# Layer norm two batches ahead computed earlier in a batch, and the loops over batches of both layers written out

## The reference, cut to what matters

```python
x = L0_attn_x                                    # (16, 512, 128)
xn = _layernorm(x, axis=-1)
x = x + _L0_attn_ref(xn, ...) + _L0_ffn_ref(xn, router_w, w_fc, w_proj, shared_fc, shared_proj)
xn = _layernorm(x, axis=-1)
x = x + _L1_attn_ref(xn, ...) + _L1_ffn_ref(xn, W_r, W_k, W_v, mu_r, mu_k)

def _layernorm(x, axis=-1, eps=1e-05):
    m = jnp.mean(x, axis=axis, keepdims=True)
    v = jnp.var(x, axis=axis, keepdims=True)
    return (x - m) / jnp.sqrt(v + eps)
```

## Time and profile before

| | us |
|---|---|
| median of 3 runs (2136.6 to 2157.64) | 2152.94 |
| the profiled execution's own time | 2159.12 |
| its span in the profile | 2157.4 |
| first layer, from the first scores of body 0 to those of body 15 | 54.2 to 699.4 |
| second layer, from the first scores of body 16 to those of body 31 | 1132.7 to 2091.8 |
| mean granted TensorE clock | 0.836 |

### The profile page before, as it was taken

One profiled execution on the slowest core, in us unless ns is written; L12 is line 12 of the kernel. 1 busy time (PEld: TensorE's weight loads), 2 busy tenths in 40 slices (PEclk: granted clock), 3 DMA queues, 4 the chain that ended last, 5 costly groups with the idle time before them and its releaser, 6 DMA issues.

```text
span 2157.4 us, 41151 instructions
## 1 busy us (share of the span) xinstructions
PE 1757.5 (81%) x13440; PEld 1049.7 (49%) x13440; DVE 1312.3 (61%) x3161; ACT 848.8 (39%) x1597; POOL 603.2 (28%) x775
## 2 busy tenths in 40 slices
PE   2788888887888699999269878888787887888895
PEld 1465556555555489999123334333333433333432
DVE  2666665566566444444276767667676667767663
ACT  1333333333333133333115444444454544444553
POOL 1554454445543312121322222112222122221000
PEclk9899998999999889999656787787787787778776
DMA  3110011101110166666352323332223332233300
GB/s 81 30 42 26 26 34 33 34 26 35 30 38 21 49 199 210 213 209 212 77 98 56 70 51 72 72 78 57 63 49 78 71 77 50 64 58 65 65 7 10
DMA packets 118025, 152.92 MB, mean 71 GB/s; under 512 B 30004, under 2 KB 82356, under 8 KB 113204
## 3 DMA queue, kind: packets, MB, share of 16 engines
q1 hardware_dynamic: 102920, 119.73, 22.4%
q0 software_dynamic: 14976, 31.49, 5.0%
HBM read 109.53 MB, written 41.62 MB: 70 GB/s over the span
## 4 chain that ended last, share of the span: by engine, by line
PE 57%; DVE 21%; issue 8%; DMA 8%; ACT 3%; SPq 1%; POOL 1%; DVEq 0%; POOLq 0%; another core or an unknown queue 0%; ACTq 0%
DVE nmax L1140 7%; PE bank L1656 7%; PE bank L1485 6%; PE bank L1610 6%; PE bank L1601 6%; DMA out<-xr 5%; PE bank L1683 5%; PE bank L1470 3%; PE bank L1451 3%; PE bank L1467 3%; PE bank L1532 3%; DVE xn L836 2%; PE bank L1631 2%; PE bank L1391 2%; DVE rope L1125 2%
## 5 line engine op out<-in xcount | busy, mean ns | idle before, releaser
L1140 DVE TENSOR_REDUCE nmax<-bank 128x1 f32<-128x512 f32 (+3 forms) x704 | 431.9, 630 | 174.4 <-PE bank L1656 159.7
L759 ACT ACTIVATE P<-bank 128x512 f32<-128x512 f32 x640 | 365.0, 597 | 343.3 <-PE bank L1683 329.7
L1656 PE MATMUL bank<-KT,QT 76*128 76x512 bf16 (+3 forms) x1024 | 328.4, 382 | 176.0 <-DVE nmax L1140 149.3
L1683 PE MATMUL bank<-QT,KT 78*128 78x512 bf16 (+3 forms) x1024 | 307.0, 383 | 8.2 <-DMA QT<-shift_d 4.2
L1656 PEld LDWEIGHTS bank<-KT,QT 76*128 76x128 bf16 x1024 | 98.1, 113 | 400.7 <-DVE nmax L1140 323.8
L528 POOL TENSOR_TENSOR P<-P,tri 128x512 f32<-128x512 f32 x128 | 160.2, 1272 | 301.0 <-ACT P L671 300.8
L1485 PE MATMUL bank<-P,V 128*32 128x512 f32 (+3 forms) x2048 | 225.2, 523 | 0.0
L1089 DVE TENSOR_TENSOR hT<-hr 128x512 f32<-128x512 f32 x144 | 99.6, 692 | 109.7 <-ACT hr L728 109.7
L1683 PEld LDWEIGHTS bank<-QT,KT 78*128 78x128 bf16 x1024 | 115.8, 119 | 99.4 <-ACT P L759 34.0
L728 ACT ACTIVATE hr<-bank 128x512 f32<-128x512 f32 x144 | 86.0, 597 | 167.5 <-PE bank L1601 167.5
L571 POOL DMA_INDIRECT hT<-ys_d,idx x128 | 129.8, 1014 | 50.5 <-issue 45.9
(11 more groups left out here) (204 smaller groups left out, 2569.3 us busy)
## 6 DMA issues: line engine op xcount, KB each, us to landing
P<-in_fc SPq DMA_DIRECT2D x72, 256.0 KB, 2.6
P<-in_proj SPq DMA_DIRECT2D x72, 256.0 KB, 2.9
QT<-parts_d SPq DMA_DIRECT2D x96, 192.0 KB
parts_d<-parts SPq DMA_DIRECT2D x32, 384.0 KB, 2.8
P<-xs_d SPq DMA_DIRECT2D x72, 128.0 KB, 2.2
ys_d<-P POOLq DMA_DIRECT2D x72, 128.0 KB, 2.7
KT<-parts_d SPq DMA_DIRECT2D x64, 128.0 KB
KT<-parts_d SPq DMA_DIRECT2D x32, 192.0 KB
```

The source lines that it names most:

```text
L759: nc.scalar.activation(P[s % 2][:, u, :], bank[k % 2][:, :], ACT.Exp, scale=float(DH) ** -0.5).then_inc(s_sb, 1)
L1140: nc.vector.tensor_reduce(nmax[:, j, h:h + nh], bank[2 + k % 2][:, 0:nh * w].rearrange("p (h w) -> p h w", h=nh), AX.X, ALU.max, negate=Tr ...
L1656: ins = pe.matmul(bank[2 + k % 2][:, i * w:(i + 1) * w], QT[n.p][0:MROWS, h, j * 128:(j + 1) * 128], KT[n.p][0:MROWS, h, 0:w], start=True, ...
L1683: ins = pe.matmul(bank[k % 2][:, c:c + n], KT[b.p][0:SROWS, h, 128 * kb:128 * kb + 128], QT[b.p][0:SROWS, h, 128 * kb:T], start=True, stop ...
```

## The change

Two things are changed. The helpers `over_batches` and `over_layer2`, which every engine uses, now write out all bodies, with known batch numbers, in place of the loops; the loop over the experts' tiles stays. And in the first layer the layer norm of batch b+2 is placed earlier in body b: `ln_moments` on DVE after `cut(b, 1)`, `ln_root` on POOL after the scatter of sheet 1, and `ln` on DVE after `y_out(b, 0)`, in front of `rotate(b + 1, 1)`. The waits stay as they were. Lines behind the helpers move up by 10.

```diff
--- before.py
+++ after.py
@@ -282,13 +282,8 @@
 
         def over_batches(eng, body):
 
-            for p in range(2):
-                body(Turn(0, p), p == 0, False)
-            with eng.Fori(1, HALVES - 1) as i:
-                for p in range(2):
-                    body(Turn(i, p), False, False)
-            for p in range(2):
-                body(Turn(HALVES - 1, p), False, p == 1)
+            for n in range(B):
+                body(Turn(n // 2, n % 2), n == 0, n == B - 1)
 
         def value(eng, v):
 
@@ -304,13 +299,8 @@
 
         def over_layer2(eng, body):
 
-            for k in range(-2, 2):
-                body(Turn(HALVES, 0) + k)
-            with eng.Fori(HALVES + 1, 2 * HALVES - 2) as i:
-                for p in range(2):
-                    body(Turn(i, p))
-            for k in range(-4, 1):
-                body(Turn(2 * HALVES, 0) + k)
+            for n in range(L2 - 2, L2 + B + 1):
+                body(Turn(n // 2, n % 2))
 
         def over_tiles(eng, body):
 
@@ -543,8 +533,8 @@
                         mask(b, s, g)
                     if s < SHEETS - 1:
                         scatter(b, range(3 * s, min(3 * s + 3, 2 * J)))
-                if not (b.known() is not None and b.known() + 2 >= B):
-                    ln_root(b + 2)
+                    if s == 1 and not (b.known() is not None and b.known() + 2 >= B):
+                        ln_root(b + 2)
 
             ln_root(Turn(0, 0))
             ln_root(Turn(0, 1))
@@ -989,22 +979,24 @@
                     y_out(b + -1, 3)
                     normalise(b + -1)
                 cut(b, 1)
+                more = not (b.known() is not None and b.known() + 2 >= B)
+                if more:
+                    dve.wait_ge(x_loaded[b.p], (b + 2).own(16, 16))
+                    ln_moments(b + 2)
                 if not last:
                     rotate(b + 1, 0)
                 cut(b, 2)
                 if not first:
                     residual(b + -1)
                 y_out(b, 0)
+                if more:
+                    ln(b + 2)
                 if not last:
                     rotate(b + 1, 1)
                     feature(b + 1)
                 cut(b, 3)
                 if not last:
                     logits_out(b + 1)
-                more = not (b.known() is not None and b.known() + 2 >= B)
-                if more:
-                    dve.wait_ge(x_loaded[b.p], (b + 2).own(16, 16))
-                    ln_moments(b + 2)
                 y_out(b, 1)
                 if not last:
                     states(b + 1)
@@ -1014,8 +1006,6 @@
                     square_h(b, k)
                 if not last:
                     slots(b + 1)
-                if more:
-                    ln(b + 2)
 
             dve.wait_ge(ready_consts, 11)
             dve.wait_ge(x_loaded[0], 16)
```

## The result

The changed kernel takes 2175.46 us, the median of 4 runs (2170.64 to 2181.88), against 2145.0 for the kernel before (4 runs, 2136.6 to 2157.64): a ratio of 1.0146 with an interval of 1.0107 to 1.0185. It is slower by about 31 us. The profiled execution took 2181.88 against 2159.12, and the two spans differ by 22.8 us, 2180.2 against 2157.4.

A forecast was written before the change was run, and what follows sets the result against it. PE, busy 81% of the span, was taken as the bound. First layer +30.5 and second layer -28.5 gave +2.0 on the profiled 2159.12, so 2161; that execution being 6.2 above the median, 2155 us, range 2125 to 2188.

The forecast's parts named there:

- the two halves cancel: Whole kernel: first layer's +30.5 us and second layer's -28.5 nearly offset, giving 2155, own range 2133 to 2174; chance 0.50.
- rival 2: First layer: last scatters share DMA engines with whole-batch transfers, landing held back 2 us; +28 us, 2183; chance 0.23.
- rival 4: Both layers: writing out brings nothing, the trace's written-out bodies being quick for another reason; 2184, up to 2207; chance 0.07.
- The boundary: First layer, between bodies: with `ln` gone from a body's end, fourteen boundaries win 2.9 us each.
- The wait: First layer, mid-body: `ln` waits for POOL's last scatter; DVE 7.0 us late, PE idle 3.9 us before `project_v`.
- A full body at full clock: First layer: a body with the early `ln` takes 40.9 + 3.8 = 44.7 us.
- The clock term: First layer: PE's partly lower clock costs 0 to 0.8 us a body; 0.5 added, giving 45.2.
- The gain of writing out ... some 24 us: First layer: written-out bodies fall from 43.3 to about 41.3 us, already contained in the 40.9 used.
- The gap of 2.8 us at a jump: Loop jumps: PE idles 19.8 / 7 each; if only five jumps count, 14 us come back, forecast 2170.
- Body 0: First layer's first body: has the delay before `ln` but no gain at its start, +6.7 us.
- The second layer: Ten loop bodies, written out, take 62.7 us instead of 65.55: -28.5, bounds -22.5 and -38.5.
- Rival 3: First layer's bodies: 2 us of slack in the later half catches up the delay; 2119 to 2129; chance 0.20.

The follow-up runs named there:

- the third buffer: The changed kernel with three instead of two buffers for `xn` in the first layer, so `ln` overwrites rows sent a body earlier: 2104.49 us, ratio 0.9771 to the kernel before.

## Why the prediction was right, and where it was wrong

The forecast was 2155 with a range of 2125 to 2188; measured is 2175.46. The range holds it, but the heart of the forecast, that the two halves cancel (2133 to 2174), doesn't. The range was that wide for the sake of rivals 2 and 4, and neither came true as it was described, so that it holds is in part luck. Of the signs of being wrong that the prediction named, one came: seven of thirteen bodies lie over 47, and the bodies are not all alike.

- **The boundary.** Right. `turn_xn` waits for `xn` nowhere, and body 14, which has only this gain, takes 38.2 instead of 41.7. That is 3.5 and not 2.9; its clock went from 0.96 to 1.00 as well.
- **The wait.** Right in place and size. `ln` started 23.7 us after the body's first scores (132.59 - 108.9); the forecast had 24.0. Its last scatter was issued 21.3 us after them (130.22), and forecast at 21.3 (118.1 - 96.8). `ln` cost 1.12, forecast 1.11. PE waited 3.1 before `project_v`, forecast 3.9. The end of phi came 28.6 after the first scores (136.85 + 0.69 - 108.9), forecast 29.3 (126.1 - 96.8).
- **A full body at full clock**, 44.7: close, but not confirmed by the six bodies of 44.7 to 44.9, which ran at 0.92 and already hold some loss by the clock. With the pause partly filled a body of this order takes 44.0 at 1.00, so the forecast was some 0.7 too high, and that the shorter bodies hit it to 0.2 is luck.
- **The clock term.** This is the step that failed: "So the clock costs between 0 and 0.8 a body; I add 0.5: 45.2." Measured is a mean of 46.3 (601.3 / 13), that is 1.6 above 44.7, outside the bounds. Against the 44.0 of a body at full clock, the six shorter ones lose 0.8 and the seven longer ones 3.5, in the mean 2.3 where 0.5 was added. The bounds came from a comparison of the loop's bodies with body 1, less the jump gaps. They took the gaps as pure loss, and body 1's clock of 1.00 as what a written-out body has. The runs with the first layer written out show that neither holds: without the gaps every body has the pause for `xn`, where in the loop 8 of 12 had it, and more time at the lower level. With PE kept at work in that pause the old order's body falls from 44.0 to 41.3, so the pause and the clock behind it cost 2.7 us there, not 0.8; its bodies at a clock of 1.00 (40.7) are 3.7 shorter than body 8 at 0.88 (44.4). In thirteen bodies the forecast is 13.7 us short (601.3 - 587.6), of the 20.8 by which it missed the difference of the spans (22.8 - 2.0).
- **"The gain of writing out ... some 24 us"** in the first layer: it is not there in the old order, where the first layer loses 10.6. The sum didn't use this number, but the 40.9 of body 1 stands behind both: its clock of 1.00 is one that the old order, written out, doesn't keep: body 1 itself has 0.89 there, and body 8 has 0.88.
- **The gap of 2.8 us at a jump** (19.8 / 7) is a misreading: three of the seven waits are 0.6 us or less, and the four long gaps have a mean of 4.7. With that mean the prediction's five jumps give back 24 us instead of 14, and its other forecast, by jumps alone, would have been 2160 instead of 2170. The sum itself didn't use it.
- **Body 0**: +10.4 instead of +6.7. With the third buffer it takes 49.0 instead of 53.0, with `ln` behind the logits 44.7, against 42.6 before. So some 4 us are the wait; the rest goes with a lower clock (0.66, 0.71 and 0.77 against 0.78), and no run took it apart.
- **The second layer**: -24.6 in all instead of -28.5, inside its bounds. The ten bodies gave 18.7, 63.7 each and not 62.7; the edges 5.9, which weren't counted.
- **The rivals.** The forecast was +2.0 us between the profiled executions, and +22.8 came. The time came out on the side of rival 2, slower by 1.5%, but not by its mechanism: `ln` began 2.4 us after the issue of the last scatter (130.22 to 132.59), where that rival needed 4.1 or more. Rival 3 is refuted by the 44.8. Rival 4 is refuted for the second layer, by the run with that layer alone written out, 0.9924. For the first layer its claim came true in the old order: writing out brought nothing, and body 1 was quick in the trace for another reason, its clock.

As the Trainium skill has it ("Runtime: NRT & Kernel Launch", section "Instruction fetch mechanics"), a taken branch to code outside the window that is held stops execution until it is fetched, one reason why kernels prefer to be written out. The first half fits this case: the four gaps of 3.7 to 5.4 us at jumps are gone with the loops, though the traces don't show that a fetch fills them. The second doesn't hold for every loop: the first layer written out alone is slower by 0.9%.

The Trainium skill's lock of the port pair ("SBUF — State Buffer", section "Who interferes with whom") fits this case in five places: the four operations of `ln` take 3.03, 2.61 and 2.06 us beside a mask of POOL, 1.11 and 1.12 without one. The traces show that `ln` is slower beside a mask, not what holds it.

## What to carry to other kernels

Before a step is moved forward, list every wait it carries and ask of each when it is met at the new place; a wait on a buffer's last reader that never cost anything can become the longest of the body. Then move it to where the last of them is met and the engine is idle anyway: behind `logits_out` instead of in front of `rotate`, with its root one sheet later, the same layer norm made the kernel 3.7% faster together with the written-out loops, instead of 1.5% slower; with the loops kept it was 1.1% faster instead of 3.0% slower. And price a pause of PE by what follows it too: body lengths that come in two sorts with two clocks point to it, and repeating harmless matmuls in the pause is a cheap test.

## What the runs showed of the hardware

- A pause of PE of about 3 us in a body of 45 to 47 us went with 7 us at the lower clock level (2 x 0.08 x 44.9) to 13 us (2 x 0.14 x 47.4). With the pause filled by repeated transposes a body was 2.7 us shorter in the mean (44.0 to 41.3), though PE did more work; bodies of that kernel take 40.7 at a granted clock of 1.00 and 44.7 at 0.89.
- A hardware loop's jump left PE idle for 3.7 to 5.4 us at four of the five jumps of the first layer, and for 0.36 us at the fifth. The kernel was 0.9% faster with this loop than with it written out; that the gaps hide the wait for `xn` fits body 4 (39.3), but was not tested by itself.
- An indirect DMA of 128 rows of 512 bytes was visible to the waiting engine 2.4 us after the start of its issue (130.22 to 132.59).
